# First scores and maxima of an attention stage moved between the feed-forward products of the stage before

## The chip, the cores and the metric

The kernel runs on one core of a Trainium2 chip. The core has five engines with a queue of instructions each: TensorE (PE in the profile; its weight loads are the rows PEld), VectorE (DVE), ScalarE (ACT), GpSimd (POOL) and SyncE (SP), which here only issues DMAs. They meet in semaphores. The metric is the device time of one execution in microseconds, as the median of several runs. Times of the trace are counted from the start of its span.

## The reference

`x` has 8 batches of 512 tokens and 128 channels. It is normalised over the channels (`xn`). One branch is causal attention with 16 heads of width 8, the other a feed-forward net that sends each half of a batch (256 tokens) through its own expert; the result is `x + s * silu(ffn)`.

```python
xn = _layernorm(x)
# attention on xn
Q, K, V = relu(xn @ Wq + bq), relu(xn @ Wk + bk), relu(xn @ Wv + bv)
scores = einsum("bqhd,bkhd->bhqk", Qh, Kh) / sqrt(8)
scores = where(sign(abs(sum(xn, -1))) == 0, NEG, scores)   # keys whose channels sum to zero
scores = where(tril == 0, NEG, scores)
s = layernorm(softmax(scores) @ Vh * query_mask + xn) * gamma + beta
# feed-forward on xn, with a layernorm of its own
x_attn = norm(xn) @ attn_w.T + attn_b + xn
h  = gelu(einsum("mend,edh->menh", x_attn, w1) + b1)       # 128 -> 512, fp32
eo = einsum("menh,ehd->mend", h, w2) + b2                  # 512 -> 128, fp32
g  = silu(gelu(eo @ next_w.T + next_b))
x + s * g
```

## The kernel before

It is written engine by engine, with every wait by hand, in two stages (two blocks). All engines meet at a barrier between the two.

**Stage one** goes over the eight batches. DVE computes the first norm exactly (`quotients`), POOL the row sums (`totals`), ACT the second norm (`second_norm`, L618). PE runs per batch the projections for Q, K and V, then eight products with `w1` (L793) and eight with `w2` (L801) in fp32, each 256 columns wide, then the transposes of the next batch (`second_normed` L725, `normed` L719) and the next product (`next_product`, L749 and L763). ACT evicts and splits Q and K into bf16 parts (`split`, `mids`), with DVE between (`rests`, `lows`); SP stores the parts to DRAM scratch and, in the loop turns 2 to 5, loads the stacks of units 0 to 3 back (`load_queries`, `load_keys`) into `q_own` and `k_own`. A **unit** is four heads of one batch; a stack holds its queries or keys with their parts, mask row and block-causality rows.

The zero masks are made once: after all sums, `masks` (DVE, three short instructions), a transpose on PE in batch 7 (L782), an ACT copy (L686), and then, on POOL's own queue, a store to DRAM and four loads of the mask row (L429, L171).

**Stage two** goes over 32 units. The maximum of each query row is needed before the exponentials. So PE first forms a unit's scores in the shape (queries, keys) in 11 chunks of at most 512 columns (`chunk`, L1224 and L1226: of `SCHUNKS` four of 384+128 columns, four of 256+128, two of 2x(128+128), one of 4x128), DVE takes the maxima of each chunk (L1059), POOL splits them (`maxima`, five short instructions L948 to L952), PE transposes them, ACT copies them (L1155), SP writes them into the stack of queries (L884). Then PE forms the scores in the shape (keys, queries) in ten chunks (`keys`, L1244 and L1246), ACT takes the exponentials (L1179), and PE multiplies by the values (`values`, L1261). Chunks of unit u+2 are laid between the `keys` of unit u, four PSUM banks deep.

For units 0 and 1 nothing stands before them. So stage two opens with their 22 chunks alone, each followed by a product that nobody reads (L1333) and that keeps PE busy. `maxima` of unit 0 follows in that row. PE begins unit 0 proper when its row of maxima has landed (`mrow_in`). Two other places have such idle products: `hold(IDLE_PRODUCTS)` with eight of them at the end of stage one (L755), and `LATE_ROWS` with six before batch 2.

## Time and profile before

| | us |
|---|---|
| median of 3 runs | 432.4 (432.21 to 433.94) |
| the profiled execution | 433.92 |
| its span (first to last instruction) | 432.2 |
| PE busy / DVE busy in the span | 371.8 / 364.4 |
| ACT busy / POOL busy | 288.2 / 205.1 |

The profiled execution is at the long end of the runs. Its span lies 1.7 us below its time. Stage one ends at about 161.4 us of the span, stage two begins there. PE is the busiest engine over the whole, but which engine ends a wait changes from stretch to stretch, so the timelines of the engines around the change are what has to be read.

### The profile page before, as it was taken

The numbers are of one execution on the slowest core, as the hardware profiler recorded it, in microseconds if no ns is written. First come the engines' busy times: TensorE is split into PE (matmuls) and PEld (weight loads), VectorE is DVE, ScalarE is ACT, GpSimd is POOL, SyncE is SP. The second block draws the span as 40 slices with busy tenths as digits, with TensorE's granted clock in tenths as the row PEclk, the third lists the DMA queues.
The fourth block names the chain that finished last, engine by engine and source line by source line (L and its number), as shares of the span: only waits on it lengthen the run. The fifth ranks groups of instructions, "written<-read, shape, count | busy, mean of one in ns | idle before, by whom it ended". The sixth has DMA issues, their size and how long they took to land.

```text
span 432.2 us, 9673 instructions
## 1 busy us (share of the span) xinstructions
PE 371.8 (86%) x3499; PEld 244.1 (56%) x3499; DVE 364.4 (84%) x846; ACT 288.2 (67%) x572; POOL 205.1 (47%) x525
## 2 busy tenths in 40 slices
PE   0046998999989989999999999999999999999960
PEld 0013676877677764566666566566566566666420
DVE  5989999999795129998999999998998989989417
ACT  0103686898878851777778788678787778778750
POOL 8532274737632032212356465374473565565592
PEclk9999899999999999999999999999999999999995
DMA  7940003564544421256533422523323233240001
GB/s 210 314 116 1 0 2 103 137 142 135 157 112 132 116 72 45 69 127 146 140 110 91 130 72 73 128 59 104 97 70 109 82 99 102 71 106 28 3 0 49
DMA packets 32407, 41.71 MB, mean 97 GB/s; under 512 B 6136, under 2 KB 24936, under 8 KB 32360
## 3 DMA queue, kind: packets, MB, share of 16 engines
q1 hardware_dynamic: 32200, 41.08, 35.1%
q8 instruction: 27, 0.44, 0.5%
q14 instruction: 20, 0.16, 0.1%
q0 software_dynamic: 160, 0.03, 0.0%
HBM read 26.43 MB, written 11.02 MB: 87 GB/s over the span
## 4 chain that ended last, share of the span: by engine, by line
PE 46%; DVE 13%; issue 2%; ACT 1%; POOL 1%; DVEq 0%; ACTq 0%; POOLq 0%
PE banks L1261 16%; PE banks L1244 9%; DVE mx L1059 8%; PE banks L1224 8%; PE banks L1226 6%; PE banks L1246 5%; DVE stats L1104 2%; PE banks L1271 2%; DVE res L1098 1%; ACT pt L1179 1%; PE banks L1233 0%; DVE res L1085 0%; DVE res L1088 0%; DVE mixed L1089 0%; DVE aggr L1108 0%
## 5 line engine op out<-in xcount | busy, mean ns | idle before, releaser
L1059 DVE TENSOR_REDUCE mx<-banks 128x1 f32<-128x512 f32 (+3 forms) x352 | 200.1, 633 | 16.7 <-PE banks L1226 15.0
L1179 ACT ACTIVATE pt<-banks 128x512 f32<-128x512 f32 x320 | 169.3, 601 | 43.7 <-PE banks L1246 36.2
L1261 PE MATMUL banks<-pt,vg 128*18 128x512 f32 (+3 forms) x1024 | 81.4, 436 | 0.7 <-ACT pt L1179 0.7
L948 POOL TENSOR_SCALAR mneg<-mx 128x16 f32<-128x16 f32 x32 | 8.1, 253 | 108.2 <-DVE mx L1059 107.0
L1224 PE MATMUL banks<-k_own,q_own 76*128 76x384 bf16 (+2 forms) x192 | 48.4, 274 | 3.3 <-DVE mx L1059 2.7
L1224 PE MATMUL banks<-w_room 76*128 76x384 bf16 (+2 forms) x192 | 48.1, 274 | 3.3 <-DVE mx L1059 3.3
L1261 PEld LDWEIGHTS banks<-pt,vg 128*18 128x18 f32 x1024 | 23.7, 97 | 43.8 <-issue 33.4
L1244 PE MATMUL banks<-w_room 76*128 76x384 bf16 (+2 forms) x192 | 47.5, 275 | 0.9 <-ACT pt L1179 0.5
L1244 PE MATMUL banks<-q_own,k_own 76*128 76x384 bf16 (+2 forms) x192 | 47.8, 274 | 0.0
L1226 PE MATMUL banks<-k_own,q_own 124*128 124x128 bf16 x256 | 44.0, 219 | 0.0
L1226 PE MATMUL banks<-w_room 124*128 124x128 bf16 x256 | 43.8, 219 | 0.0
L1246 PE MATMUL banks<-q_own,k_own 124*128 124x128 bf16 x256 | 42.5, 219 | 0.0
L1246 PE MATMUL banks<-w_room 124*128 124x128 bf16 x256 | 42.2, 219 | 0.0
L755 PE MATMUL banks<-bias_rows,ones_p 128*128 128x512 bf16 x36 | 10.6, 457 | 27.9 <-DVEq L511 27.9
L793 PE MATMUL banks<-xaT,w_room 128*128 128x256 f32 x128 | 29.2, 381 | 0.8 <-ACT xaT L636 0.8
L801 PE MATMUL banks<-hid,w_room 128*128 128x256 f32 x128 | 28.9, 379 | 0.0
L693 ACT ACTIVATE hid<-banks,cols_sb 128x256 f32<-128x256 f32 x64 | 26.8, 470 | 1.5 <-PE banks L793 0.9
L1244 PEld LDWEIGHTS banks<-w_room 76*128 76x128 bf16 x192 | 18.7, 97 | 14.8 <-ACT pt L1179 6.8
L1224 PEld LDWEIGHTS banks<-k_own,q_own 76*128 76x128 bf16 x192 | 18.4, 97 | 14.4 <-DVE mx L1059 8.9
L793 PEld LDWEIGHTS banks<-xaT,w_room 128*128 128x128 f32 x128 | 23.7, 190 | 5.0 <-ACT xaT L636 2.0
L801 PEld LDWEIGHTS banks<-hid,w_room 128*128 128x128 f32 x128 | 24.3, 190 | 3.3
L1244 PEld LDWEIGHTS banks<-q_own,k_own 76*128 76x128 bf16 x192 | 18.7, 97 | 12.5 <-issue 3.4
(199 smaller groups left out, 736.4 us busy)
## 6 DMA issues: line engine op xcount, KB each, us to landing
k_scratch<-parts SPq DMA_DIRECT2D x40, 128.0 KB, 2.3
k_own<-k_scratch SPq DMA_DIRECT2D x48, 96.0 KB
w_room<-k_scratch SPq DMA_DIRECT2D x48, 96.0 KB
q_scratch<-parts SPq DMA_DIRECT2D x24, 128.0 KB, 2.3
q_own<-q_scratch SPq DMA_DIRECT2D x32, 96.0 KB
w_room<-q_scratch SPq DMA_DIRECT2D x32, 96.0 KB
w_room<-in_w_dram SPq DMA_DIRECT2D x1, 2048.0 KB, 12.5
q_own<-q_scratch SPq DMA_DIRECT2D x16, 112.0 KB
```

The lines of the kernel that those rows point to most:

```text
L693: ins = act.activation(hid[:, h, j, :], banks[:, bank + j // 2, EC * (j % 2):EC * (j % 2) + EC], ACT.Gelu, bias=b1[2 * n + h][j])
L755: mm(banks[:, TRX, :], ones_p[:, :], bias_rows[:, 0:1, :].broadcast_to([P, TB, C]), start=True, stop=True)
L793: ins = mm(banks[:, bank + j // 2, EC * (j % 2):EC * (j % 2) + EC], w1_sb[:, 2 * n + h, P * j:P * j + P], xaT[:, EC * h:EC * h + EC], star ...
L801: ins = mm(banks[:, XB, EC * h:EC * h + EC], w2_sb[:, 2 * n + h, j, :], hid[:, h, j, :], start=(j == 0), stop=(j == HC - 1))
L1059: dve.tensor_reduce(mx[:, u % 2, heads[0]:heads[-1] + 1, q], banks[:, S0 + slots[0] % SLOTS, 0:w * len(heads)].rearrange("p (h k) -> p h k ...
L1104: ins = dve.bn_stats(stats[:, k, :], res[:, k, :])
L1179: act.activation(pt[:, T * j:T * j + T], banks[:, bank(), :], ACT.Exp, scale=SCALE).then_inc(exp_done, 1)
L1224: mm(o[:, 0:w - P], qx[by][0:LIVE, g, h, P * q:P * q + P], kx[by][0:LIVE, g, h, 0:w - P], start=True, stop=True)
L1226: ins = mm(o[:, w - P:w], qx[by][0:STACK, g, h, P * q:P * q + P], kx[by][0:STACK, g, h, w - P:w], start=True, stop=True)
L1244: mm(o[:, P:n], kx[par][0:LIVE, g, h, P * k:P * k + P], qx[par][0:LIVE, g, h, P * k + P:T], start=True, stop=True)
L1246: ins = mm(o[:, 0:P], kx[par][0:STACK, g, h, P * k:P * k + P], qx[par][0:STACK, g, h, P * k:P * k + P], start=True, stop=True)
L1261: ins = mm(banks[32 * h:32 * h + VP, OT, P * k:T], vg[:, g, k, h, :], pt[:, KPLACE[k, h]:KPLACE[k, h] + n], start=(k == 0 and g % 2 == 0), ...
```

## The change

- The 11 chunks of unit 0 now stand in batch 6 of stage one, those of unit 1 in batch 7, one behind each of eleven of the sixteen feed-forward products (`FIRST_PLACES`). They use two banks in turn, those of the transposes (`FIRST_BANKS`), so from the third chunk on each waits until the maxima of the chunk two before are taken. PE waits before the products of each of these batches for the unit's stacks with its mask row.
- DVE takes their maxima (`first_maxima`) behind its last norms: all of unit 0 before `lows` of batch 6, three of unit 1 before `rests` of batch 7, eight after it.
- The masks are made in two halves. The first half (batches 0 to 3) is made on DVE in loop turn 4, transposed in batch 5, and stored and loaded by SP in turn 4, which waits there for the store. The second half is stored by POOL in the end.
- Stage two opens with eight idle products and `maxima` of unit 0. POOL clears and fills the values after `maxima(0)` instead of ahead of it.

PE around the products of batch 6. `banks<-xaT,w_room` are the products with `w1`, `banks<-hid,w_room` those with `w2`. Before:

```order
L736 MATMUL banks<-wv_sb,xnT 128x128 x4
L793 MATMUL banks<-xaT,w_room 128x256 x8
L801 MATMUL banks<-hid,w_room 128x256 x8
L725 MATMUL banks<-ident,xl_st 128x128 x4
L719 MATMUL banks<-ident,xn_all 128x128 x4
```

After, the same place up to the third chunk (the names `k_own,q_own` are the scores of units 0 and 1):

```order
L763 MATMUL banks<-wv_sb,xnT 128x128 x4
L844 MATMUL banks<-xaT,w_room 128x256 x2
L796 MATMUL banks<-k_own,q_own 128x384
L798 MATMUL banks<-k_own,q_own 128x128
L844 MATMUL banks<-xaT,w_room 128x256
L796 MATMUL banks<-k_own,q_own 128x384
L798 MATMUL banks<-k_own,q_own 128x128
L844 MATMUL banks<-xaT,w_room 128x256
L796 MATMUL banks<-k_own,q_own 128x384
L798 MATMUL banks<-k_own,q_own 128x128
```

The row of eight products has been opened up, and short bf16 products stand between the fp32 ones; batch 7 reads alike.

DVE at the end of stage one, from its last `lows` inside the loop on (`parts` is `lows`, `rest` is `rests`, `mx` the maxima). Before:

```order
L560 TENSOR_TENSOR parts<-rest,parts 128x2x512
L554 TENSOR_TENSOR rest<-full,parts 128x1024
L547 TENSOR_SCALAR zero_all<-small 128x32
L548 TENSOR_SCALAR live_all<-zero_all 128x32
L549 TENSOR_SCALAR mask_b<-zero_all 128x32
L560 TENSOR_TENSOR parts<-rest,parts 128x2x512
L554 TENSOR_TENSOR rest<-full,parts 128x1024
L560 TENSOR_TENSOR parts<-rest,parts 128x2x512
L603 MEMSET banks 128x512
```

After:

```order
L560 TENSOR_SCALAR mask_b<-zero_all 128x16
L568 TENSOR_REDUCE mx<-banks 128x1 x8
L568 TENSOR_REDUCE mx<-banks 128x2 x2
L568 TENSOR_REDUCE mx<-banks 128x4
L581 TENSOR_TENSOR parts<-rest,parts 128x2x512
L568 TENSOR_REDUCE mx<-banks 128x1 x3
L575 TENSOR_TENSOR rest<-full,parts 128x1024
L568 TENSOR_REDUCE mx<-banks 128x1 x5
L568 TENSOR_REDUCE mx<-banks 128x2 x2
L568 TENSOR_REDUCE mx<-banks 128x4
L581 TENSOR_TENSOR parts<-rest,parts 128x2x512
L630 MEMSET banks 128x512
```

The 22 reductions that opened stage two have come in behind `rests` of batch 6.

SP in loop turn 4 of stage one, after:

```order
L272 DMA k_scratch<-parts 16x8x512 x5
L162 DMA q_own<-q_scratch 24x2048 x2
L162 DMA q_own<-q_scratch 28x2048
L168 DMA k_own<-k_scratch 24x2048 x3
L303 DMA mask_scratch<-maskT 16x128
L174 DMA k_own<-mask_scratch 1x4x512 x4
L264 DMA q_scratch<-parts 16x8x512 x3
```

The mask's store and its four loads are new between the loads of unit 2 and the stores of batch 5; before, they stood on POOL.

The diff, without declarations, renumberings and what follows from moved names:

```diff
@@ -51,6 +51,8 @@
 BIG = 2.0 ** 100
 HELD = 22
 LATE_ROWS = {2: 6}
+MASKED = (B // 2 + 1, B - 1)
+FIRST_PLACES = ((1, 2, 3, 5, 6, 7), (1, 2, 4, 5, 6))
 IDLE_PRODUCTS = 8
 SCALE = float(DH) ** -0.5
 RSQRT_SEED = 0x5F3759DF
@@ -289,6 +298,12 @@
                     if 2 <= i < 2 + NG:
                         load_queries(sp, 0, 0, i - 2)
                         load_keys(sp, 0, 0, i - 2)
+                    if i == B // 2:
+                        sp.wait_ge(maskT_ready, 1)
+                        sp.dma_start(mask_dram[0:NT // 2, :], maskT[:, 0]).then_inc(mask_out, 16)
+                        sp.wait_ge(mask_out, 16)
+                        for g in range(NG):
+                            load_mask(sp, 0, 0, g, stack_in[0][g])
             @block.gpsimd
             def _(pool):
                 pool.memset(ident[:, :], 0.0).then_inc(blank, 1)
@@ -425,14 +440,9 @@
                         first_roots(tok, GROUPS[1])
                     if i == 4:
                         first_roots(tok, GROUPS[2])
-                pool.wait_ge(maskT_ready, 1)
-                pool.dma_start(mask_dram, maskT[:, :]).then_inc(mask_out, 16)
-                pool.wait_ge(mask_out, 16)
-                for g in range(NG):
-                    load_mask(pool, 0, 0, g, mask_in)
-                pool.wait_ge(mask_in, 16 * NG)
-                for g in range(NG):
-                    pool.sem_inc(stack_in[0][g], 16)
+                pool.wait_ge(maskT_ready, 2)
+                pool.dma_start(mask_dram[NT // 2:NT, :], maskT[:, 1]).then_inc(mask_in, 16)
+                pool.wait_ge(mask_in, 16)
 
                 pool.sem_inc(blank, -10)
 
@@ -541,12 +551,23 @@
                     dve.tensor_reduce(s16[:, tiles, :], xn_all[:, tiles, :].rearrange("p n (k l) -> p n l k", l=16),
                                       AX.X, ALU.add).then_inc(lanes_ready, 1)
 
-                def masks():
-
-                    dve.wait_ge(sums_ready, B)
-                    link(dve.tensor_scalar(zero_all[:, :], rem[:, :], 0.0, None, ALU.is_equal))
-                    link(dve.tensor_scalar(live_all[:, :], zero_all[:, :], -1.0, 1.0, ALU.mult, ALU.add))
-                    dve.tensor_scalar(mask_b[:, :], zero_all[:, :], -BIG, None, ALU.mult).then_inc(mask_ready, 1)
+                def masks(part):
+
+                    at = slice(NT // 2 * part, NT // 2 * (part + 1))
+                    dve.wait_ge(sums_ready, B // 2 * (part + 1))
+                    link(dve.tensor_scalar(zero_all[:, at], rem[:, at], 0.0, None, ALU.is_equal))
+                    link(dve.tensor_scalar(live_all[:, at], zero_all[:, at], -1.0, 1.0, ALU.mult, ALU.add))
+                    dve.tensor_scalar(mask_b[:, at], zero_all[:, at], -BIG, None, ALU.mult).then_inc(mask_ready, 1)
+
+                def first_maxima(tok, u, chunks):
+
+                    for c in chunks:
+                        q, heads = SCHUNKS[c]
+                        w = P * (q + 1)
+                        dve.wait_ge(first_done, tok.next(first_done))
+                        dve.tensor_reduce(mx[:, u, heads[0]:heads[-1] + 1, q],
+                                          banks[:, FIRST_BANKS[c % 2], 0:w * len(heads)].rearrange(
+                                              "p (h k) -> p h k", k=w), AX.X, ALU.max).then_inc(first_free, 1)
 
                 def rests(tok, i):
 
@@ -596,9 +617,15 @@
                     if i == 1:
                         dve.wait_ge(x_in[2], 16)
                         statistics(GROUPS[1])
-                masks()
+                    if i == B // 2:
+                        masks(0)
+                masks(1)
+                first_maxima(tok, 0, range(NS))
                 lows(tok, B - 2)
+                first_maxima(tok, 1, range(3))
                 rests(tok, B - 1)
+                first_maxima(tok, 1, range(3, NS))
+                dve.wait_ge(first_free, AHEAD * NS)
                 lows(tok, B - 1)
                 link(dve.memset(banks[:, OT, :], 0.0))
                 dve.wait_ge(rows_in, 16)
@@ -755,6 +782,23 @@
                         mm(banks[:, TRX, :], ones_p[:, :], bias_rows[:, 0:1, :].broadcast_to([P, TB, C]),
                            start=True, stop=True)
 
+                def first_chunk(u, c):
+
+                    if c == 1:
+                        pe.wait_ge(maskT_ready, u + 1)
+                    if c > 1:
+                        pe.wait_ge(first_free, NS * u + c - 1)
+                    q, heads = SCHUNKS[c]
+                    w = P * (q + 1)
+                    for k, h in enumerate(heads):
+                        o = banks[:, FIRST_BANKS[c % 2], w * k:w * k + w]
+                        if q > 0:
+                            mm(o[:, 0:w - P], qx[0][0:LIVE, u, h, P * q:P * q + P], kx[0][0:LIVE, u, h, 0:w - P],
+                               start=True, stop=True)
+                        ins = mm(o[:, w - P:w], qx[0][0:STACK, u, h, P * q:P * q + P],
+                                 kx[0][0:STACK, u, h, w - P:w], start=True, stop=True)
+                    ins.then_inc(first_done, 1)
+
                 def next_product():
 
                     pe.wait_ge(eoT_ready, tok.next(eoT_ready))
@@ -777,10 +821,17 @@
                     n = i % STEPS
                     if i > 0:
                         projections(tok, i)
-                    if i == B - 1:
-                        pe.wait_ge(mask_ready, 1)
-                        pe.transpose(banks[:, TRX, :].bitcast(BF16)[0:NT, 0:P], mask_b[:, :],
+                    if i in MASKED:
+                        part = MASKED.index(i)
+                        pe.wait_ge(mask_ready, part + 1)
+                        pe.transpose(banks[:, TRX, :].bitcast(BF16)[0:NT // 2, 0:P],
+                                     mask_b[:, NT // 2 * part:NT // 2 * (part + 1)],
                                      ident_b[:, :]).then_inc(maskT_done, 1)
+                    ahead = i >= B - AHEAD
+                    if ahead:
+                        u = i - (B - AHEAD)
+                        pe.wait_ge(fixed_in[0][u], 48)
+                        pe.wait_ge(stack_in[0][u], UNIT_DMAS)
                     pe.wait_ge(xaT_ready, tok.next(xaT_ready))
                     if i == 0:
                         pe.wait_ge(w_ffn_in, 32)
@@ -795,12 +846,19 @@
                                      start=True, stop=True)
                             if j % 2 == 1:
                                 ins.then_inc(h_done, 1)
+                            if ahead and HC * h + j in FIRST_PLACES[0]:
+                                first_chunk(u, FIRST_PLACES[0].index(HC * h + j))
                     for h in range(2):
                         pe.wait_ge(hid_ready, tok.next(hid_ready))
                         for j in range(HC):
                             ins = mm(banks[:, XB, EC * h:EC * h + EC], w2_sb[:, 2 * n + h, j, :],
                                      hid[:, h, j, :], start=(j == 0), stop=(j == HC - 1))
-                    ins.then_inc(eo_done, 1)
+                            if h == 1 and j == HC - 1:
+                                ins.then_inc(eo_done, 1)
+                            if ahead and HC * h + j in FIRST_PLACES[1]:
+                                first_chunk(u, len(FIRST_PLACES[0]) + FIRST_PLACES[1].index(HC * h + j))
+                    if ahead and i < B - 1:
+                        pe.wait_ge(first_free, NS * (u + 1))
                     if i < B - 1:
                         hold(LATE_ROWS.get(i + 1, 0))
                         second_normed(tok, i + 1)
@@ -808,6 +866,7 @@
                     next_product()
                     if i < B - 1:
                         attn_product(tok, i + 1)
+                pe.wait_ge(first_free, AHEAD * NS)
                 hold(IDLE_PRODUCTS)
 
 
@@ -943,7 +999,8 @@
 
                 def maxima(u):
 
-                    pool.wait_ge(s_free, released(u))
+                    if u >= AHEAD:
+                        pool.wait_ge(s_free, released(u))
                     part = [mparts[:, u % 2, G * TB * p:G * TB * (p + 1)] for p in range(PARTS)]
                     link(pool.tensor_scalar(mneg[:, 0], mx[:, u % 2].rearrange("p h n -> p (h n)"), -1.0, None, ALU.mult))
                     link(pool.tensor_copy(part[0], mneg[:, 0]))
@@ -1027,13 +1084,13 @@
                         pool.wait_ge(out_stored, 16 * b)
                         pool.sem_inc(factors_ready, 1)
 
+                link(pool.memset(mparts[:, :, :], 0.0))
+                tok = Tokens(pool)
+                maxima(0)
                 link(pool.memset(vg[:, :, :, :, :], 0.0))
                 for g in range(NG):
                     values_in(0, g)
-                link(pool.memset(mparts[:, :, :], 0.0))
-                tok = Tokens(pool)
-                for u in range(2):
-                    maxima(u)
+                maxima(1)
                 for b in range(B):
                     batch(tok, b)
 
@@ -1136,9 +1193,6 @@
                 dve.sem_inc(s_free, SLOTS)
                 dve.sem_inc(res_free, 1)
                 tok = Tokens(dve)
-                for u in range(2):
-                    for c in range(NS):
-                        chunk(tok, u, c)
                 for b in range(B):
                     batch(tok, b)
 
@@ -1325,15 +1384,10 @@
                         outputs(tok)
 
                 tok = Tokens(pe)
-                for u in range(2):
-                    pe.wait_ge(fixed_in[0][u], 48)
-                    pe.wait_ge(stack_in[0][u], tok.next(stack_in[0][u], UNIT_DMAS))
-                    for c in range(NS):
-                        chunk(tok, 0, u, c)
-                        mm(banks[:, ST0 + RING - 1, :], qx[0][0:LIVE, u, 0, 0:P], kx[0][0:LIVE, u, 0, :],
-                           start=True, stop=True)
-                        if (u, c) == (1, 5):
-                            maxima(tok, 0)
+                for u in range(AHEAD):
+                    tok.next(stack_in[0][u], UNIT_DMAS)
+                hold(IDLE_PRODUCTS)
+                maxima(tok, 0)
                 for b in range(B):
                     batch(tok, b)
 
```

## Rows read from the trace of the kernel before

**Rows 1.** First line of the page.

```profile
span 432.2 us, 9673 instructions
```

**Rows 2.** PE in batches 6 and 7: start us, us, engine, line, operation [idle before].

```profile
136.16 3.62 PE L793 MATMUL banks<-xaT,w_room 128*128 128x256 f32 x16
139.62 3.62 PE L801 MATMUL banks<-hid,w_room 128*128 128x256 f32 x16
143.07 0.60 PE L725 MATMUL banks<-ident,xl_st 128*128 128x128 f32 x4
...
149.92 0.23 PE L782 MATMUL banks<-ident_b,mask_b 128*32 128x128 bf16 x1
150.08 3.72 PE L793 MATMUL banks<-xaT,w_room 128*128 128x256 f32 x16
153.63 3.62 PE L801 MATMUL banks<-hid,w_room 128*128 128x256 f32 x16
158.18 0.39 PE L749 MATMUL banks<-bias_rows,ones_p 128*128 128x512 bf16 x1 [0.93 <-ACT eoT L703]
...
159.30 1.89 PE L755 MATMUL banks<-bias_rows,ones_p 128*128 128x512 bf16 x8
```

**Rows 3.** DVE in batch 6: `rests` and the first instruction of the masks.

```profile
136.92 1.22 DVE L554 TENSOR_TENSOR rest<-full,parts 128x1024 f32<-128x1024 f32 x1 [2.30 <-ACT parts L658]
138.18 0.18 DVE L547 TENSOR_SCALAR zero_all<-small 128x32 f32<-128x32 f32 x1
```

**Rows 4.** First instruction of stage two on PE, same columns.

```profile
161.63 0.32 PE L1224 MATMUL banks<-k_own,q_own 76*128 76x384 bf16 x1 [0.45 <-DVEq L1136]
```

**Rows 5.** The chain of waits: start us, us, what; DVE's maxima of units 0 and 1.

```profile
162.05 12.19 DVE mx L1059 x22
```

**Rows 6.** Opening of stage two on POOL, up to the split of unit 0's maxima.

```profile
161.44 1.06 POOL L1030 MEMSET vg<- 128x1152 f32 x1 [5.40 <-POOLq L265]
...
163.58 0.30 POOL L1033 MEMSET mparts<- 128x256 bf16 x1
168.37 0.27 POOL L948 TENSOR_SCALAR mneg<-mx 128x16 f32<-128x16 f32 x1 [4.49 <-DVE mx L1059]
```

**Rows 7.** The same on SP: last store of batch 7's queries, write of the maxima.

```profile
163.36 0.59 SPq L256 DMA_DIRECT2D q_scratch<-q_fixed  x1
170.44 6.69 SPq L884 DMA_DIRECT2D q_own<-mT  x2
```

**Rows 8.** PE at the start of unit 0, inside it, and at the start of unit 1.

```profile
172.72 0.34 PE L1224 MATMUL banks<-k_own,q_own 76*128 76x384 bf16 x1
...
172.95 0.33 PE L1244 MATMUL banks<-q_own,k_own 76*128 76x384 bf16 x1
...
175.77 0.23 PE L1233 MATMUL banks<-ident_b,mparts 128*128 128x128 bf16 x1 [0.54 <-POOL mparts L952]
...
178.17 1.49 PE L1261 MATMUL banks<-pt,vg 128*18 128x512 f32 x16
...
180.04 0.33 PE L1224 MATMUL banks<-k_own,q_own 76*128 76x384 bf16 x1
```

**Rows 9.** The wait ahead of batch 6's transposes, from POOL over ACT to PE.

```profile
121.54 1.09 POOL L404 TENSOR_TENSOR s<-s 128x32 f32<-128x32 f32 x1 [4.72 <-DVE s L541]
126.23 1.65 ACT L618 ACTIVATE xl_st<-xn_all,shift,small 128x128 f32<-128x128 f32 x4 [2.77 <-POOLq L411]
127.93 0.88 PE L725 MATMUL banks<-ident,xl_st 128*128 128x128 f32 x4 [1.90 <-ACT xl_st L618]
```

**Rows 10.** One microsecond behind it: PE, PEld, DVE, ACT, POOL busy, then PEclk, DMA.

```profile
129.00:130.00 1.00, 1.00 (x6) 0.85 (x5) 0.96 (x4) 0.93 (x2) 0.00 (x0) 0.50 0.81 206
```

**Rows 11.** POOL: the wait between the mask's store and its loads.

```profile
154.01 2.03 POOL L171 DMA_DIRECT2D k_own<-mask_scratch  x4 [1.86 <-DMA mask_scratch<-maskT]
```

**Rows 12.** SP's queue at turns 4 and 5: end of the loads, begin of the stores.

```profile
129.74 1.18 SPq L165 DMA_DIRECT2D k_own<-k_scratch  x3
134.65 2.12 SPq L255 DMA_DIRECT2D q_scratch<-parts  x3
```

27 lines of the change are left out of this document (17 added, 10 removed).

## The prediction

> **What bounds the kernel now.** I read the page first, then the timelines of all five engines around the border of the stages, then windows for the clock. The profiled execution took 433.92 us: a span of 432.2 [rows 1] and 1.7 around it. Three parts of it matter.
>
> Stage one, batches 6 and 7, is bound by PE. Its sixteen fp32 products of a batch take from 136.16 to 143.07, 0.43 us each and back to back [rows 2]. DVE idles there: it waits 2.30 us for ACT before `rests` [rows 3].
>
> The opening of stage two is bound by DVE. PE starts at 161.63 [rows 4], and DVE takes the 22 maxima in one piece of 12.19 us, 0.55 each [rows 5]. Unit 0 can't start when its own eleven are done: POOL splits them from 168.37 on [rows 6], SP writes them at 170.44 [rows 7], and PE starts unit 0 at 172.72 [rows 8], 11.1 us after the stage began. This is what the change attacks: it moves work from a place where DVE is the limit into one where DVE idles. But in the new place PE is the limit, and every chunk costs PE time there. The question is the balance.
>
> Third, between batches 5 and 6 PE waits 1.90 us for the second norm, which waits for POOL's sums, which wait for DVE [rows 9]. What delays DVE before that point delays all.
>
> **What stage two gains.** If it began at the same time, POOL would clear `mparts` at 161.44 (0.30) and go straight on. From POOL's first step to SP's write is 170.44 - 168.37 = 2.07, so the maxima would be ready at 163.9. SP is free of its stores at 163.36 + 0.59 = 163.95 [rows 7], so it holds nobody up. From the write to PE's start is 172.72 - 170.44 = 2.28. Unit 0 starts at 166.3 instead of 172.72: **-6.4**. ACT's table for the exponentials is still loaded in the time of that write.
>
> Unit 0 itself: it took 180.04 - 172.72 = 7.3. PE's work in it is 21 groups (11 chunks, 10 `keys`) of 0.23 at most (172.95 - 172.72 is one chunk of 512 columns) = 4.8, and a `values` part of 1.4 [rows 8], 6.2 in all. The rest is DVE's backlog and POOL's late split of unit 1 (0.54 in one wait). Both are gone when 22 maxima lie behind. **-1.1**. POOL's clearing and filling of `vg` now stands ahead of `maxima(1)`, but it is 2.1 us of work begun in PE's idle time, and costs nothing.
>
> The clock, on the other side. Before, PE was kept busy up to 172.7. Now it has eight idle products (1.7 us, by the row of the eight at 159.30 in [rows 2]), one transpose, and then nothing until the write lands: from 163.4 to 166.3, 2.9 us. Behind the wait of 1.90 us the granted clock was 0.50, which is 1.2 GHz [rows 9, 10]. What a low stretch costs: from the transposes to the first product took 136.16 - 127.93 = 8.2 with it, and 149.92 - 143.07 = 6.85 without [rows 2, 9]: 1.4. I take 1.2, as some of it may fall into the idle time, and 0 to 1.5 as bounds: **+1.2**.
>
> **What stage one pays.** The first half of the masks: three short DVE instructions of 0.18 and their gaps [rows 3], in loop turn 4, ahead of the norms of batches 5 and 6, which are on the path of rows 9. **+0.6**. The mask transpose of batch 5 on PE falls into the 1.90 us wait and is free. It shortens that wait, and the low clock behind it may go: the three runs before are 432.4, 433.9 and 432.2, the profiled one is 433.9, and the 1.5 between them is the price of such a stretch. So I take 432.4 as the time without it and sum against that. Before, batch 6 would then begin its products at 134.7.
>
> The chunks on PE. Seven of eleven have 512 columns (0.23), four have 384 (0.17): 2.3 per unit, **+4.6** for two. All of it is on the path.
>
> The price of standing between fp32 products. The trace has one such insertion, the mask transpose at 149.92. The eight products with `w1` behind it take 153.63 - 150.08 = 3.55, against 139.62 - 136.16 = 3.46 without: 0.09, the weight load that a short product does not cover. The whole insertion, with its own start behind a wait, pushed the products about 0.35 back for 0.06 of columns, so 0.29 is the upper bound, and 0 the lower. Most chunks find their semaphore long set, so I take the 0.09: 22 x 0.09 = **+2.0** (0 to 6.4).
>
> The Trainium skill ("TensorE: Matmul & The Clock Gate", section "Step-by-step: what each phase is for") says that weight loads are pulled ahead of matmuls in flight, so that the next tile's weights load while this one runs. By that rule the 2.0 would be 0 and the forecast 433.3; the 0.09 and the 0.29 of this trace speak against it for short products.
>
> Waits in batch 6. The half mask: SP ends its loads of turn 4 at 129.74 + 1.18 = 130.9, with the 0.6 at 131.5. It then stores the mask and waits. POOL idled 1.86 us behind the issue of that store [rows 11], so some 2.3 pass to the release; the load of unit 0's mask row takes 2.3 more (as the write of rows 7): 136.2. PE, at 134.7 + 0.6 = 135.3, waits 0.9. If the low stretch stays, PE comes at 136.8 and needn't wait, but then the third chunk waits for the first maximum: `rests` ends at 138.1 + 0.6, the masks at 139.4, the maximum at 140.0, and PE is there at 138.9. Either way **+1.0**. Queued behind SP's wait are four mask loads (2.0 [rows 11]) and the stores of batch 5, due at 134.65 + 0.6 [rows 12] and now 0.7 later; ACT needs them out only in batch 7. After that DVE keeps up: a chunk and a product take PE over 0.7 us, a maximum 0.55.
>
> The end of batch 6: the transposes write the chunks' banks and wait for the last maximum, which starts 0.2 behind its chunk, lasts 0.6 and has one product of 0.43 as cover: **+0.35**. In batch 7, `rests` (1.22) stands between the third and the fourth maximum, and the sixth chunk waits: **+0.4**. The new semaphore waits before the products: **+0.2**. Hidden: the maxima, `lows` and the clearing of the output bank end on DVE before PE's last idle products; POOL's mask store (second half) has over 10 us.
>
> Sum for stage one: 0.6 + 4.6 + 2.0 + 1.0 + 0.35 + 0.4 + 0.2 = 9.2. Stage two gives 6.4 + 1.1 - 1.2 = 6.3 back. Net +2.9: **435.3 us**. The work is the same as before, but in stage one it is added at PE's full price, and in stage two the chain POOL, PE, ACT, SP, DMA of 4.7 us stays uncovered.
>
> **The rivals.** *The clock stays up* in the 2.9 us gap. For it: whether a gap lowers the clock seems to differ between runs (432.4 against 433.9 with the same wait). Against: the gap is longer than the 1.90. Price -1.2: 434.1.
>
> *The insertions are nearly free.* The weight loads hide, and the clock stays up. For it: in stage two chunk follows on `keys` without a gap [rows 8]; against it the 0.09. 432.4 + 9.2 - 2.0 - 7.5 = 432.1, no slower than before. With the low clock it decides at about 0.06 per insertion: below, the time is within 0.5%.
>
> *The insertions cost what the mask transpose did.* Each chunk stands behind a semaphore wait of its own. 22 x 0.20 more = 4.4, of which some 1.0 takes the place of waits for DVE: 438.7.
>
> *The mask row comes late.* SP's store queues behind the stores and loads of turn 4. If release and load take 3.3 instead of 2.3 each, PE stands 2.0 longer and the clock falls there: 437.3.
>
> **How the numbers follow.** Forecast as summed 0.46 (its own range 434.0 to 436.6), clock stays up 0.16, insertions free 0.14, insertions dear 0.12, mask late 0.08; 0.04 for a gain in stage two that I don't see. What a measurement can tell from no change is about 0.5%, 2.2 us: slower begins at 434.6, faster at 430.2. Slower: three quarters of the forecast (0.35), 0.06 of the clock case, both dear ones (0.20), 0.61 together. Within: 0.11 + 0.10 + 0.12 = 0.33. Faster: 0.06. The range of 432.0 to 438.2 leaves out half of the free case, most of the dear one and the unseen gain, 0.18.
>
> **What would show it.** Right: the first `keys` of unit 0 some 4.7 us behind the start of stage two, that start at about 170.8 less 1.5 if the low stretch is gone, unit 0 at 6.2 (or 7.5 and PEclk 0.50 right behind the gap); the products of batch 6 and their chunks from first to last 10.2 to 11 us against 6.9; a wait of about 1 us ahead of them or in front of the third chunk. Wrong: pitch of a 384+128 chunk between fp32 products at 0.23 or at 0.5; PE waiting for the mask beyond 2 us; DVE running behind PE in batch 7; or DVE's norms of batches 5 and 6 not 0.6 later.

## The result and the profile after

| | before | after |
|---|---|---|
| median, us | 432.6 (432.21 to 433.94, 4 runs) | 436.46 (436.29 to 436.94, 4 runs) |
| ratio | | 1.0085, 95% interval 1.0062 to 1.0109 |
| the profiled execution / its span | 433.92 / 432.2 | 436.29 / 434.5 |
| start of stage two on PE | 161.63 | 168.32 |
| start of unit 0 | 172.72 | 173.11 |
| start of unit 1 | 180.04 | 182.39 |

The changed kernel is 3.9 us slower, by the interval 2.7 to 4.7. Two executions stand far outside all others and enter no ratio below: one of the kernel before (2102.99 us) and one of the kernel with later masks (735.48 us). From unit 1 on, the two profiled executions run alike: 252.2 us are left before, 252.1 after. So the start of unit 1 is the yardstick for everything below. Between the two profiles it moved by 2.35 us only, since the profile of before carries the low clock stretch ahead of batch 6 [rows 10] and that of after does not carry it there.

PE after, columns as in [rows 2]; L752 are the transposes, L844 and L796 products with `w1` and chunks, L1287 the idle products at the opening of stage two, L1278 the first chunk of a unit, L1320 `values`:

```profile
128.59 0.66 PE L752 MATMUL banks<-ident,xl_st 128*128 128x128 f32 x4 [1.15 <-ACT xl_st L645]
...
136.37 1.10 PE L844 MATMUL banks<-xaT,w_room 128*128 128x256 f32 x4 [1.04 <-issue]
...
146.68 0.66 PE L752 MATMUL banks<-ident,xl_st 128*128 128x128 f32 x4 [0.30 <-DVE mx L568]
...
153.51 1.13 PE L844 MATMUL banks<-xaT,w_room 128*128 128x256 f32 x4
...
158.93 0.28 PE L796 MATMUL banks<-k_own,q_own 76*128 76x256 bf16 x1 [0.36 <-DVE mx L568]
...
168.32 1.89 PE L1287 MATMUL banks<-k_own,q_own 76*128 76x512 bf16 x8 [0.30 <-PEq L274]
...
173.11 0.34 PE L1278 MATMUL banks<-k_own,q_own 76*128 76x384 bf16 x1 [2.75 <-DMA q_own<-mT]
...
179.89 2.11 PE L1320 MATMUL banks<-pt,vg 128*18 128x512 f32 x16
...
182.39 0.33 PE L1278 MATMUL banks<-k_own,q_own 76*128 76x384 bf16 x1
```

Against [rows 2, 4, 8, 9]: batch 6, from the first product to the next transposes, takes 10.31 us for 6.91. Stage two reaches unit 0 in 4.79 us for 11.09. But unit 0 then takes 9.28 us for 7.32, although the same instructions are in it and DVE has no backlog any more. The windows behind the gap say why (columns as in [rows 10]; the first row answers to that of before):

```profile
129.00:130.00 1.00, 1.00 (x11) 0.96 (x10) 0.96 (x5) 0.97 (x3) 0.00 (x0) 1.00 0.76 202
...
174.00:175.00 1.00, 1.00 (x9) 0.67 (x8) 1.00 (x3) 1.00 (x3) 0.00 (x0) 0.68 0.00 0
175.00:176.00 1.00, 1.00 (x9) 0.76 (x7) 0.88 (x2) 0.83 (x2) 0.00 (x0) 0.50 0.00 0
...
180.00:181.00 1.00, 1.00 (x8) 0.23 (x11) 0.26 (x1) 0.59 (x1) 0.00 (x0) 0.50 0.86 170
```

PE is full in each. The granted clock (the value after POOL's) was 0.50, which is 1.2 GHz, from 174.4 to 181.2 us, for 6.8 us. PE had stood idle for 2.75 us until 173.11 and worked for 1.3 us before the clock fell. The `values` part of [rows 8] took 1.49 us, here 2.11.

SP after, in turn 4 and at the opening of stage two (L303 stores the mask half, L174 loads the mask rows, L940 writes the maxima):

```profile
131.65 0.35 SPq L303 DMA_DIRECT2D mask_scratch<-maskT  x1
134.32 2.55 SPq L174 DMA_DIRECT2D k_own<-mask_scratch  x4
...
170.23 0.61 SPq L265 DMA_DIRECT2D q_scratch<-q_fixed  x1
170.88 0.80 SPq L940 DMA_DIRECT2D q_own<-mT  x1
```

The release of the mask's store took 2.67 us, and PE's first product of batch 6 waited for the first of the loads behind it: that is the 1.04 us, which the timeline calls "issue" (the run with the early store, below, makes it go). The maxima were copied by 170.67 and SP was free at 170.84, so its stores held the write by 0.2 us, which the prediction had ruled out.

DVE around the masks' first instruction: `rest` stands ahead of it, `quo` opens the next batch's norm. Before, then after:

```profile
96.74 1.27 DVE L554 TENSOR_TENSOR rest<-full,parts 128x1024 f32<-128x1024 f32 x1
98.04 0.69 DVE L524 TENSOR_TENSOR quo<-xn_all,small 128x512 f32<-128x512 f32 x1
```

```profile
96.89 1.27 DVE L575 TENSOR_TENSOR rest<-full,parts 128x1024 f32<-128x1024 f32 x1
98.19 0.17 DVE L558 TENSOR_SCALAR zero_all<-small 128x16 f32<-128x16 f32 x1
...
98.73 0.68 DVE L534 TENSOR_TENSOR quo<-xn_all,small 128x512 f32<-128x512 f32 x1
```

`quo` starts 0.69 us later than before, and the transposes of batch 6 0.66 us later (128.59 for 127.93). Of that, 0.15 us were there ahead of the masks; the masks themselves take 0.54 (98.19 to 98.73).

### The profile page after: what moved, and what is told of

Read it like the earlier page. It is cut to its first block, busy times and chain, and to the rows that moved or that the text cites. A ratio compares the mean times of both kernels' runs of the same rounds, so it can differ in the third digit from the quotient of the medians.

```text
span 434.5 us, 9650 instructions
## 1 busy us (share of the span) xinstructions
PE 371.3 (85%) x3486; PEld 244.4 (56%) x3486; DVE 367.0 (84%) x849; ACT 288.9 (66%) x573; POOL 202.9 (47%) x521
## 4 chain that ended last, share of the span: by engine, by line
PE 47%; DVE 10%; issue 2%; ACT 1%; SPq 1%; DMA 1%; POOL 0%; DVEq 0%; ACTq 0%; POOLq 0%
PE banks L1320 16%; PE banks L1303 9%; PE banks L1278 9%; PE banks L1280 6%; PE banks L1305 6%; DVE mx L1116 6%; DVE stats L1161 2%; PE banks L1330 2%; DVE res L1155 1%; ACT pt L1233 1%; DMA q_own<-mT 1%; SPq L264 0%; PE banks L1292 0%; DVE res L1142 0%; DVE res L1145 0%
## 5 line engine op out<-in xcount | busy, mean ns | idle before, releaser
L1116 DVE TENSOR_REDUCE mx<-banks 128x1 f32<-128x512 f32 (+3 forms) x330 | 188.5, 634 | 22.0 <-PE banks L1280 20.0
L1320 PE MATMUL banks<-pt,vg 128*18 128x512 f32 (+3 forms) x1024 | 82.0, 438 | 0.7 <-ACT pt L1233 0.7
L1278 PE MATMUL banks<-w_room 76*128 76x384 bf16 (+2 forms) x192 | 48.1, 274 | 3.3 <-DVE mx L1116 3.3
L1303 PE MATMUL banks<-q_own,k_own 76*128 76x384 bf16 (+2 forms) x192 | 48.8, 280 | 0.0
L1320 PEld LDWEIGHTS banks<-pt,vg 128*18 128x18 f32 x1024 | 23.7, 97 | 44.4 <-issue 34.0
L1278 PE MATMUL banks<-k_own,q_own 76*128 76x384 bf16 (+2 forms) x168 | 43.2, 281 | 5.3 <-DMA q_own<-mT 2.8
L1280 PE MATMUL banks<-k_own,q_own 124*128 124x128 bf16 x224 | 39.2, 223 | 0.0
L844 PE MATMUL banks<-xaT,w_room 128*128 128x256 f32 x128 | 31.5, 386 | 1.8 <-issue 1.0
L854 PE MATMUL banks<-hid,w_room 128*128 128x256 f32 x128 | 31.2, 384 | 0.0
L1305 PEld LDWEIGHTS banks<-q_own,k_own 124*128 124x128 bf16 x256 | 25.6, 100 | 1.1
L844 PEld LDWEIGHTS banks<-xaT,w_room 128*128 128x128 f32 x128 | 22.9, 190 | 5.9 <-ACT xaT L663 1.6
L419 POOL TENSOR_TENSOR s<-s 128x32 f32<-128x32 f32 x8 | 7.7, 958 | 38.8 <-DVE s L551 38.8
```

Of the source, the lines that this page charges most:

```text
L844: ins = mm(banks[:, bank + j // 2, EC * (j % 2):EC * (j % 2) + EC], w1_sb[:, 2 * n + h, P * j:P * j + P], xaT[:, EC * h:EC * h + EC], star ...
L854: ins = mm(banks[:, XB, EC * h:EC * h + EC], w2_sb[:, 2 * n + h, j, :], hid[:, h, j, :], start=(j == 0), stop=(j == HC - 1))
L1116: dve.tensor_reduce(mx[:, u % 2, heads[0]:heads[-1] + 1, q], banks[:, S0 + slots[0] % SLOTS, 0:w * len(heads)].rearrange("p (h k) -> p h k ...
L1278: mm(o[:, 0:w - P], qx[by][0:LIVE, g, h, P * q:P * q + P], kx[by][0:LIVE, g, h, 0:w - P], start=True, stop=True)
L1280: ins = mm(o[:, w - P:w], qx[by][0:STACK, g, h, P * q:P * q + P], kx[by][0:STACK, g, h, w - P:w], start=True, stop=True)
L1303: mm(o[:, P:n], kx[par][0:LIVE, g, h, P * k:P * k + P], qx[par][0:LIVE, g, h, P * k + P:T], start=True, stop=True)
```

## The experiments

Each was compared with the kernel before on the same chip. In most comparisons the times of before fall into two groups, some 1.5 us apart; in that of the last row they run from 432.44 to 434.42 without a clear gap. Where kernels of different comparisons are set side by side, I take the distance to the median of the times up to 433.2, called the lower group: 432.40, 432.60, 432.37, 432.45 and 432.88 in the five comparisons. It is a yardstick between rows, not a cost: a kernel's own median holds slower executions too, and the yardstick itself moves by 0.5 us between comparisons.

| | median, us | ratio to before (95%) | to the lower group | start of unit 1 |
|---|---|---|---|---|
| after | 436.46 | 1.0085 (1.0062 to 1.0109) | +4.1 | 182.39 |
| kept busy | 433.9 | 1.0004 (0.9989 to 1.0018) | +1.3 | 181.01 |
| masks later | 437.34 | 1.0084 (1.0062 to 1.0105) | +4.7 | |
| early mask store | 436.6 | 1.0067 (1.0048 to 1.0086) | +4.0 | 183.03 |
| one unit ahead | 429.54 | 0.9903 (0.9883 to 0.9923) | -3.1 | 175.62 |
| one unit, masks in turn 4 | 430.41 | 0.9935 (0.9912 to 0.9957) | -2.0 | 177.36 |
| kept busy, masks later | 432.92 | 1.0002 (0.9987 to 1.0016) | +0.6 | 178.66 |
| the same, early mask store | 432.68 | 0.9987 (0.9974 to 1.0001) | +0.3 | 178.02 |
| one unit, early write | 429.63 | 0.9922 (0.9899 to 0.9946) | -2.7 | 175.74 |
| before, kept busy | 432.73 | 0.9988 (0.9972 to 1.0003) | +0.3 | 178.31 |
| before, kept busy, 22 more idle products | 437.4 (one run) | | +5.0 | 183.45 |
| rest of the change | 433.03 | 1.0001 (0.9988 to 1.0013) | +0.6 | 178.82 |
| one unit, wide product last | 429.9 | 0.9924 (0.9909 to 0.9939) | -3.0 | 176.32 |

The starts of unit 1 are of one profiled execution each and contain its low clock stretches in stage one, which fall differently in each.

**The clock behind the gap.** Theory: the low clock is what made unit 0 long. Idle products fill the gap.

```diff
                 hold(IDLE_PRODUCTS)
                 maxima(tok, 0)
+                for _ in range(13):
+                    mm(banks[:, S0, :], qx[0][0:LIVE, 1, 0, 0:P], kx[0][0:LIVE, 1, 0, :], start=True, stop=True)
```

> The changed kernel with 13 more idle products on PE (2.8 us) behind the transpose of unit 0's maxima, so that PE is busy until the write of the maxima lands. Theory: after the idle gap of 2.75 us the granted clock was 0.50 for 6.8 us, and unit 0 took 9.28 us from its first chunk to that of unit 1 instead of the 6.2 that its products need; the gap costs 3.1. Then unit 0 takes 6.2 to 6.5, PEclk stays 1.00 and the time is 433.4. Rival: unit 0 is held by ACT's exponentials or by the maxima whatever the clock; then it still takes 8 us or more and the time stays within 1 us of the changed kernel, 435.5 to 436.5.

433.9 (12 runs). PE at the opening of stage two:

```profile
169.75 1.89 PE L1287 MATMUL banks<-k_own,q_own 76*128 76x512 bf16 x8 [0.30 <-PEq L274]
171.63 2.97 PE L1392 MATMUL banks<-k_own,q_own 76*128 76x512 bf16 x13
174.54 0.34 PE L1278 MATMUL banks<-k_own,q_own 76*128 76x384 bf16 x1
```

And the window in which the clock had fallen after the change (the same place in unit 0; the clock is 1.00 in every window from 171 to 179):

```profile
175.00:176.00 1.00, 1.00 (x11) 0.71 (x10) 1.00 (x2) 0.81 (x2) 0.00 (x1) 1.00 0.00 0
```

Unit 0 starts 4.79 us into the stage, exactly as without the idle products, and ends at 181.01: 6.47 us for 9.28. The clock cost 2.8 us in that profile; the medians differ by 2.6 us, the distances to the lower group by 2.8. No other edit with two units ahead gave back as much, and the rival (unit 0 is held by the exponentials or the maxima whatever the clock) falls.

**The masks' place.** The three instructions one turn later, behind the norms on the path.

```diff
-                    if i == B // 2:
+                    if i == B // 2 + 1:
                         masks(0)
```

> The changed kernel with DVE's first half of the masks one loop turn later, behind rests of batch 4, where DVE waits 2.66 us for POOL's roots. Theory: the three instructions delayed everything by 0.66 us through the norms; now they are free, batch 6's transposes start 0.6 earlier, and so do SP's stores, its mask loads and the end: 435.8. Rival: the norms are not the path, or PE's wait for the mask row takes the 0.66 back: 436.3 to 436.6.

No gain: 437.34. Its only trace is of the execution of 735.48 us and is not read, so no row shows its clock behind the gap. So I asked again where the clock is kept up, and in the kernel with one unit ahead.

> The changed kernel with 13 idle products behind the transposes of unit 0's maxima in stage two (no low clock there), and the first half of the masks one loop turn later. It asks why the later masks alone gained nothing. Theory: the clock hid it, the 0.66 us are there once the clock is even: 433.2, against 433.9 with the idle products alone. Rival: PE's wait for the mask row ahead of the products of batch 6 takes them back, since the mask's transpose moves with DVE's work and the row lands no sooner: 433.9.

> The variant with only unit 0's chunks in stage one, but with the first half of the masks on DVE back in loop turn 4, where the changed kernel has it. One part differs. Theory: the three instructions stand ahead of the norms of batches 5 and 6, which are on the path; the changed kernel's trace had them 0.66 us late. So 0.6 to 0.7 more than the variant's 429.5: 430.2. Rival: as in the pair of the changed kernel with and without that shift (436.4 and 437.3), the place of the masks makes no difference or turns against the late place: 429.5 or less.

With one unit ahead the later place gives 1.1 us (-3.1 for -2.0 to the lower group; ratios 0.9903 and 0.9935, whose intervals overlap). With the clock kept up it is 0.75 by the lower group but 0.1 by the ratios (1.0002 for 1.0004), and each ratio is known to 0.6 us only. The traces agree with each other: from the start of `rest` in turn 4 (the row at 96.89 above) to the transposes of batch 6 they take 31.70 to 31.74 us in the five profiles with the masks in turn 4, and 31.13 to 31.16 us in the five with the later masks. So the masks cost 0.5 to 0.6 us. The missing gain of the first run is not explained. Its mean granted clock is 0.970, that of the changed kernel 0.9725, which would be 2.2 us more at the lower level (0.0025 x 436 / 0.5); but single executions of the two range from 0.964 to 0.976, so this shows nothing for certain.

**The mask row.** SP stores the mask half ahead of its turn's stores, and waits for it where it did.

```diff
                     sp.wait_ge(low_ready, tok.next(low_ready))
+                    if i == B // 2:
+                        sp.wait_ge(maskT_ready, 1)
+                        sp.dma_start(mask_dram[0:NT // 2, :], maskT[:, 0]).then_inc(mask_out, 16)
                     store_queries(sp, i)
```

> The changed kernel with the mask's store on SP ahead of the stores of batch 4 instead of behind its loads, and SP's wait for it where it was: it has long landed, so the mask row of unit 0 should land 2.3 us earlier and PE's wait of 1.04 us before batch 6's products goes. Theory: the wait moves to the third chunk, which needs the first maximum, and that starts only at 137.73 behind rests and the masks: about 0.9 of the 1.04 comes back as a wait there, the time is 436.2. Rival: the wait was a cost of its own: 435.4.

436.6. The wait ahead of the products is gone, and in the third chunk PE now waits for DVE's first maximum, as the theory had it:

```profile
138.41 0.34 PE L797 MATMUL banks<-k_own,q_own 76*128 76x384 bf16 x1 [0.84 <-DVE mx L569]
```

One wait takes the place of the other, 0.84 for 1.04. (Unit 0 took 10.23 us in this profile, from 172.80 to 183.03: the low clock lasted longer there than after the change.) With clock and masks mended as well:

> The one before with SP's store of the first mask half ahead of the stores of its loop turn; the wait for it stays behind the loads. Theory: the mask row lands over a microsecond before PE is there, so the wait ahead of the products of batch 6 is gone, and a wait of some 0.8 us for the first maximum, seen in the run with the early store alone, takes most of its place: 0.2 to 0.3 less than without, about 433.0. Rival: nothing is left to gain, 433.2 to 433.9, or SP's later stores are pushed back and ACT waits for its buffers in batch 7: above 434.

432.68, the best that I found with two units ahead: all its mended parts together bring it to the kernel before, not below. Its third chunk waits 0.72 us:

```profile
137.16 0.34 PE L797 MATMUL banks<-k_own,q_own 76*128 76x384 bf16 x1 [0.72 <-DVE mx L569]
```

**What is left without the chunks.** The changed kernel with `AHEAD = 0`: the 22 chunks open stage two as before, and masks in halves, SP's loads of the mask rows and POOL's new order remain.

> The changed kernel with no unit ahead: all 22 chunks open stage two as before, with their idle products. What is left of the change are the masks in two halves (first half on DVE in loop turn 4, stored and loaded by SP), POOL's maxima(0) ahead of its clearing and filling of the values, and unit 0's write. It prices all that the chunks do not. Theory: 0.66 for the masks ahead of the norms, nothing for the rest, as DVE's row of maxima bounds the opening: 0.6 over the kernel before, a ratio of 1.0015. Rival: the later filling of the values or SP's waiting row takes something too: 1 us or more over.

433.03: +0.6 to the lower group, which is what the masks cost (by the ratio it is no different from before). POOL's order costs nothing that shows. PE takes 11.06 us to unit 0 and 7.36 in it, before 11.09 and 7.32:

```profile
160.40 0.32 PE L1278 MATMUL banks<-k_own,q_own 76*128 76x384 bf16 x1 [0.48 <-DVEq L1190]
...
171.46 0.34 PE L1278 MATMUL banks<-k_own,q_own 76*128 76x384 bf16 x1
...
178.82 0.33 PE L1278 MATMUL banks<-k_own,q_own 76*128 76x384 bf16 x1
```

**One unit ahead.** If every chunk costs PE its full price in stage one, the second unit's are the ones to leave out: in stage two they can cover the chain that brings unit 0's maxima.

The edit, shortened:

```diff
-    AHEAD = 2
+    AHEAD = 1
@@ DVE, stage two
+                for c in range(NS):
+                    chunk(tok, 1, c)
@@ PE, stage two
-                hold(IDLE_PRODUCTS)
-                maxima(tok, 0)
+                pe.wait_ge(fixed_in[0][1], 48)
+                pe.wait_ge(stack_in[0][1], tok.next(stack_in[0][1], UNIT_DMAS))
+                for c in range(NS):
+                    chunk(tok, 0, 1, c)
+                    mm(banks[:, ST0 + RING - 1, :], qx[0][0:LIVE, 1, 0, 0:P], kx[0][0:LIVE, 1, 0, :],
+                       start=True, stop=True)
+                    if c == 5:
+                        maxima(tok, 0)
```

(The masks are made in turn 5, and unit 0's chunks stand in batch 7.)

> Only unit 0's chunks are moved into stage one, into batch 7; unit 1's chunks and maxima open stage two again with their idle products between, the transpose of unit 0's maxima behind the sixth of them, and the first half of the masks is made one loop turn later. Theory: stage one pays once (3.4 us in batch 7, nothing in batch 6), the chain of 4.8 us from POOL to the landed maxima is covered by unit 1's chunks, the clock stays up, unit 0 starts 4.8 to 5.0 us into stage two instead of 11.1: before + 3.4 - 6.2 - 0.3 = 429.5, faster than both kernels. Rival: DVE's 6.0 us of maxima for unit 1 reach beyond the chain and hold back unit 0 as much as the 11.1 did: 432 to 433.

429.54, better than both kernels. Its PE at the opening of stage two:

```profile
163.24 0.32 PE L1279 MATMUL banks<-k_own,q_own 76*128 76x384 bf16 x1 [0.45 <-DVEq L1192]
...
169.16 0.34 PE L1279 MATMUL banks<-k_own,q_own 76*128 76x384 bf16 x1 [0.95 <-DMA q_own<-mT]
...
175.62 0.33 PE L1279 MATMUL banks<-k_own,q_own 76*128 76x384 bf16 x1
```

And SP there, its last store and the write of the maxima:

```profile
166.26 0.60 SPq L265 DMA_DIRECT2D q_scratch<-q_fixed  x1
166.90 0.82 SPq L939 DMA_DIRECT2D q_own<-mT  x1
```

Against the kernel before with its wait ahead of batch 6 filled (last experiment; stage two at 159.90, unit 1 at 178.31): stage one pays 3.3 us, the opening gives 5.2 (5.92 for 11.09), unit 0 gives 0.9 (6.46). The second unit, in the changed kernel, makes the opening only another 1.1 us shorter, costs another 5.1 of stage one (3.4 in batch 6, 1.04 of waiting, 0.5 to 0.6 for the masks), and leaves PE nothing to do in the gap, which brings the clock's 2.8.

SP's write stood behind its stores here, and PE waited 0.95 us. I sent it ahead of them, and the transpose of the maxima one chunk sooner.

> The variant with only unit 0's chunks in stage one, and two things earlier in the opening of stage two: the transposes of unit 0's maxima one chunk sooner on PE, and SP's write of them ahead of the stores of the last batch's queries. In the variant's trace SP issued the write at 166.90 behind stores that ended at 166.86, and PE waited 0.95 us for it at 169.16. Theory: the write goes out at about 165.7 and the wait is gone, but unit 1's maxima then hold the first ring of banks: some 0.6 of it is gained, 428.9. Rival: DVE's backlog takes all of it, 429.5; or the late stores hold ACT's last buffers, over 430.

PE inside unit 0, from its fifth chunk to the start of unit 1:

```profile
170.58 0.28 PE L1279 MATMUL banks<-k_own,q_own 76*128 76x256 bf16 x1 [0.19 <-DVE mx L1115]
...
171.47 0.23 PE L1293 MATMUL banks<-ident_b,mparts 128*128 128x128 bf16 x1 [0.55 <-POOL mparts L1008]
...
175.74 0.33 PE L1279 MATMUL banks<-k_own,q_own 76*128 76x384 bf16 x1
```

The wait for the write is gone, unit 0 starts at 168.44, 5.07 us into the stage for 5.92. But unit 1 starts 12.37 us into it, where it was 12.38. DVE's row of 21 maxima lasts 11.6 us in both, and PE meets it inside unit 0 instead of before it. 429.63: the rival was right, DVE takes all. In all four kernels with one unit ahead, unit 1 starts 12.36 to 12.38 us into the stage, however the opening and unit 0 share them.

**The price of an insertion.** The kernel before with idle products of 512 columns at the chunks' eleven places in batch 6, five of them among the products with `w2`, and the same eleven in one row in batch 5 (the wait ahead of batch 6 is filled, as in the last experiment). The edit, without its part for the products with `w2`:

```diff
                             if j % 2 == 1:
                                 ins.then_inc(h_done, 1)
+                            if i == B - 2 and HC * h + j in (1, 2, 3, 5, 6, 7):
+                                hold(1)
+                    if i == B - 3:
+                        hold(11)
```

> The one before this with 22 more idle bf16 products of 512 columns: in batch 6 one behind each of eleven of the sixteen feed-forward products, at the places of the changed kernel's chunks; in batch 5 the same eleven in one row, between the products with w1 and those with w2. It measures the price of standing between fp32 products by itself, inside one trace. Theory of the prediction: 0.09 per insertion, so batch 6 takes 6.9 + 11 x (0.22 + 0.09) = 10.3 us from the first to the last product, batch 5 6.9 + 11 x 0.22 + 0.09 = 9.4. What the changed kernel's trace reads: 0.05 to 0.06 per insertion, 9.9 against 9.4. Rival, weight loads run ahead in full: 9.3 in both.

PE in batch 5 (one row) and batch 6 (inserted); L793 and L805 are the fp32 products, L755 the idle ones:

```profile
119.44 3.62 PE L793 MATMUL banks<-xaT,w_room 128*128 128x256 f32 x16
122.90 2.54 PE L755 MATMUL banks<-bias_rows,ones_p 128*128 128x512 bf16 x11
...
128.73 2.10 PE L755 MATMUL banks<-bias_rows,ones_p 128*128 128x512 bf16 x9
...
137.19 1.03 PE L793 MATMUL banks<-xaT,w_room 128*128 128x256 f32 x4
...
146.47 0.60 PE L725 MATMUL banks<-ident,xl_st 128*128 128x128 f32 x4
```

9.29 in a row (119.44 to 128.73) and 9.28 inserted (137.19 to 146.47): a product of 512 columns between fp32 products costs its columns and nothing else. The chunks do cost more. The changed kernel's rows, at the first chunk of batch 7:

```profile
154.48 0.33 PE L796 MATMUL banks<-k_own,q_own 76*128 76x384 bf16 x1
154.64 0.22 PE L798 MATMUL banks<-k_own,q_own 124*128 124x128 bf16 x1
154.70 0.65 PE L844 MATMUL banks<-xaT,w_room 128*128 128x256 f32 x2
155.19 0.33 PE L796 MATMUL banks<-k_own,q_own 76*128 76x384 bf16 x1
```

The chunk takes 0.22 (154.48 to 154.70), the fp32 product behind it 0.49 where it is 0.43 elsewhere, so 0.05 an insertion. What differs is what stands last: 128 columns, 0.06 us. So the next run turned the two products of a chunk round.

> The variant with only unit 0's chunks in stage one (first half of the masks later), with the two products of a chunk in the other order: the 128 columns of the diagonal first, the 384 or 256 columns last. In the traces of the changed kernel and of this variant the first pass of the fp32 product behind a chunk takes 0.27 us instead of 0.216, and behind an idle product of 512 columns it takes 0.216. Theory: the fp32 weights load beside the product ahead, and 128 columns (0.06 us) are too short to cover them. With 256 or 384 columns ahead the 0.053 is gone behind eight of the eleven chunks and stays behind the three that end in 128 columns: 0.43 us in all, 429.1 for 429.5. Rival: what costs is the change of type or of row count, whatever stands last, or the short product now exposes the load of its own successor: the passes behind chunks still take 0.27, or the chunks grow by as much, 429.5.

PE in batch 7, L794 the 124 rows with the diagonal and L797 the 76 rows, which stand last:

```profile
150.30 0.33 PE L797 MATMUL banks<-k_own,q_own 76*128 76x384 bf16 x1
150.46 0.60 PE L843 MATMUL banks<-xaT,w_room 128*128 128x256 f32 x2
150.90 0.22 PE L794 MATMUL banks<-k_own,q_own 124*128 124x128 bf16 x1
...
154.58 0.23 PE L794 MATMUL banks<-k_own,q_own 124*128 124x128 bf16 x1 [0.52 <-DVE mx L568]
...
157.44 0.22 PE L797 MATMUL banks<-k_own,q_own 76*128 76x128 bf16 x1
157.50 0.65 PE L853 MATMUL banks<-hid,w_room 128*128 128x256 f32 x2
157.98 0.22 PE L794 MATMUL banks<-k_own,q_own 124*128 124x128 bf16 x1
```

The fp32 product behind 384 columns takes 0.44 (150.46 to 150.90), and the chunk didn't grow. Where the last product has 76 rows too but only 128 columns, the fp32 product behind it still takes 0.48 (157.50 to 157.98). So the price hangs on the columns of the product that stands last, not on its rows or on the change of type. That it is the weight load which a short product leaves uncovered fits this, but no run shows the load by itself. The Trainium skill ("TensorE: Matmul & The Clock Gate", section "Step-by-step: what each phase is for") says that the next tile's weights load while this one's matmul runs; the trace agrees behind 384 and 512 columns and shows 0.05 us left over behind 128. The median didn't move (429.9, ratio 0.9924 for 0.9903). Of the 0.43 expected, 0.16 went into the wait for DVE at the sixth chunk, which grew from 0.36 to 0.52; the other 0.3 are too little for these comparisons to show.

**The low stretch of the kernel before.**

```diff
-LATE_ROWS = {2: 6}
+LATE_ROWS = {2: 6, 6: 9}
```

> The kernel before with nine idle products in PE's wait of 1.90 us ahead of the transposes of batch 6 (a table entry; nothing else differs). The prediction took this wait for the cause of the low granted clock that began at 128.22 us in the profiled run, and that stretch for the 1.5 us between the two groups of the kernel before's times (432.4 to 432.9, and 433.7 to 434.8 in the first comparison of these runs). Theory: no low stretch at 128, and the times gather in the lower group, 432.0 to 432.9. Rival: the low stretches fall elsewhere in stage one too (one trace had one at 72, others at 38 to 53), the two groups stay, and the median is 433.3 to 434.0.

PE, the transposes and the first product of batch 6:

```profile
127.84 0.66 PE L725 MATMUL banks<-ident,xl_st 128*128 128x128 f32 x4
...
134.42 3.62 PE L793 MATMUL banks<-xaT,w_room 128*128 128x256 f32 x16
```

From the transposes to the first product PE takes 6.58 us, with the low stretch 8.23 [rows 2, 9]: the stretch costs 1.65 us. The two groups did not go away: 9 of 12 times lie at 432.95 or below, three from 433.27 to 434.07, and 10 of 23 of the kernel before lie at 433.2 or below. The median is 0.7 us lower, the ratio 0.9988 with 1 inside its interval. Low stretches in other traces lie at 38 to 53 and at 72 us of stage one, so this wait can be one cause of the upper group, not all of it. How large its part is stays open: the prediction had taken this stretch for the whole 1.5 us between the executions.

## Why the prediction was right where it was, and where it wasn't

It said 435.3 and slower; measured was 436.46, inside the range. The mechanism held: what the move costs PE in stage one is more than what it takes off the opening. Two of its terms were off, in opposite directions, so that the sum came this close is in part luck. Taken against a profile of before without its low stretch (1.65 us off 161.63 and what follows), the path moved like this:

| term | predicted | measured |
|---|---|---|
| masks of turn 4 on DVE | +0.6 | +0.5 to 0.6 |
| wait ahead of the products of batch 6 | +1.0 | +1.04 |
| columns of 22 chunks | +4.6 | +4.5 (0.225 for 512 columns, 0.173 for 384) |
| 22 insertions | +2.0 | +1.2 (22 x 0.053) |
| last maximum of batch 6 | +0.35 | +0.3 to 0.5 |
| sixth chunk of batch 7 | +0.4 | +0.4 to 0.6 |
| semaphore waits, mask transpose | +0.2 | +0.2 |
| stage one in all | +9.2 | +8.3 |
| to unit 0 | -6.4 | -6.3 |
| unit 0, backlog | -1.1 | -0.85 |
| unit 0, clock | +1.2 | +2.8 (3.8 in the profile with the early mask store) |
| net | +2.9 | +4.0 |

The measured terms of stage one are read one by one and add up to 8.4; the 8.3 is the start of stage two, 168.32, less 161.63 - 1.65.

**The balance held.** Moving the chunks takes DVE's row of 12.19 us off the opening and puts PE's full price into batches where PE is the bound. The chain behind the maxima (4.7 us predicted, 4.79 measured) stays uncovered. Both came as worked out.

**The insertions were priced too high.** The step took 0.09 from the mask transpose, a product of 128 columns ahead of the fp32 products, and used it for chunks. The chunks show 0.053, and nothing once their widest product stands last, which fits the cause given there, a weight load that a short product doesn't cover. Why the mask transpose, with 128 columns as well, costs more than a chunk stays open: it is one sample, and in batch 6 of the changed kernel, where a wait and no transpose stands ahead, the first two fp32 products already take 0.93 (136.37 to 137.30) where two take 0.86 elsewhere. The rival of dear insertions (0.29 each, 438.7) falls with the 0.053.

**The clock was the term furthest off.** The step priced the stretch behind the gap like the one ahead of batch 6, and even took something off for time that might be idle. The stretch here was 6.8 us long, twice that of before (3.4), all of it in PE's full work, and cost 2.8, outside the bounds of 0 to 1.5. They should have been open above: one row of one low stretch says what that stretch cost, not how long the next will be.

**The rivals.** That the clock stays up is what the idle products make true: 433.9, where the prediction had 434.1 for it. The insertions free (432.1) fell: they cost 1.2 in all and the clock 2.8. The late mask row didn't happen: release 2.67 us, where 2.3 was taken and 3.3 was the rival's. "SP is free of its stores, so it holds nobody up" was wrong by 0.2 us.

## What to carry to other kernels

Work that is moved from an engine's bottleneck into another's should be moved only as far as it buys something: the first unit's 11 chunks shortened the opening by 5.2 us for 3.3, the second's by 1.1 for 5.1, since by then a chain of transfers set the time and the chunks had been its cover. Before emptying such a row, ask what PE will do while the chain runs, and give it idle products if nothing else is there. Between fp32 products, a chunk that ends in its widest product saves 0.05 us an insertion; with eleven insertions that showed in the trace, not in the time.

## What the runs showed of the chip

- A gap of 2.75 us on PE was followed by 6.8 us at 1.2 GHz under full work, and in the run with the early mask store a gap of 2.74 us in the same place came with 10.2 us (171.43 to 181.67). A gap of 1.90 us ahead of batch 6 was followed by 3.4 us in one profile [rows 9, 10]; waits of 1.43 to 1.56 us in the same place were followed by none in seven others.
- The length of the gap alone doesn't decide. A gap of 2.64 to 2.67 us ahead of 70 to 71 us stands in eight profiles: in four the clock fell for 3.4 us from about 72 us on, in the other four it stayed at 1.00. A gap of 1.42 or 1.43 us ahead of 41 to 42 us stands in ten, and a second of 1.15 us close behind; in five of these the clock fell within 2.2 us of the first, in five it didn't.
- In the profiles of these kernels, which do the same work up to 96 us, the low stretches differ: 3.4 or 10.2 us long, beginning near 38, 43 or 72 us, one, two or none.
- Thirteen idle products in the gap delayed nothing and saved 2.6 us by the medians, 2.8 by the distances to the lower group.
